# Branch sum, its norm, the output product, the residual and the third norm by halves of the tokens, in a macaron layer on one Trainium2 core

## What is computed

```
x = x + 0.5 * FFN(layernorm(x))
x = x + attention(layernorm(x))
x = x + 0.5 * FFN(layernorm(x))
```

```
w = softmax(logits / t); w = max(w, floor); w = w / w.sum(-1)
o = sum(w[..., i:i+1] * branches[i] for i in range(4))
o = o * rsqrt((o * o).mean(-1) + 1e-5) * onorm_w
x = x + o.reshape(b, l, 256) @ Wo
# then layernorm(x), the third norm, and the second FFN
```

## Time and profile before

| | us |
|---|---|
| median of 3 runs | 1204.77 (1200.77 to 1204.84) |
| the profiled execution | 1207.12 |
| its span, first to last instruction | 1205.4 |
| PE busy | 1053.0 (87%) |
| DVE busy | 821.7 (68%) |
| ACT busy | 548.9 (46%) |
| POOL busy | 414.4 (34%) |

### The profile page before, as it was taken

The page is one execution under the profiler, slowest core; times in us unless marked ns, Lnnn a source line. Parts: engine busy times, 40 slices in busy tenths (PEclk is TensorE's granted clock), DMA queues, the critical chain, the costliest instruction groups (busy, mean ns, idle before and its releaser), DMA issues.

```text
span 1205.4 us, 25681 instructions
## 1 busy us (share of the span) xinstructions
PE 1053.0 (87%) x10348; PEld 779.9 (65%) x10348; DVE 821.7 (68%) x1556; ACT 548.9 (46%) x965; POOL 414.4 (34%) x648
## 2 busy tenths in 40 slices
PE   3938898899989998899988998899988998897738
PEld 2823784488637884488637885488637885487427
DVE  6584477875787577875787667865787567863363
ACT  2244338443655337443564337443564337532322
POOL 8118200950058200951048300861048300860000
PEclk9968899999999999999999999999999999995758
DMA  5140104020220103020230203110130202120000
GB/s 156 19 105 2 35 18 96 11 52 2 69 55 11 43 19 89 18 48 6 51 74 3 51 19 73 33 35 20 44 80 1 53 1 68 39 51 3 1 0 18
DMA packets 82933, 47.45 MB, mean 39 GB/s; under 512 B 58496, under 2 KB 76416, under 8 KB 82816
## 3 DMA queue, kind: packets, MB, share of 16 engines
q1 hardware_dynamic: 82816, 45.82, 16.4%
HBM read 31.12 MB, written 14.68 MB: 38 GB/s over the span
## 4 chain that ended last, share of the span: by engine, by line
PE 59%; DVE 25%; ACT 7%; issue 4%; POOL 3%; DMA 1%; SPq 0%; DVEq 0%; ACTq 0%; POOLq 0%
PE psum L789 12%; PE psum L791 11%; PE psum L790 11%; DVE conv_acc L1374 6%; PE psum L820 4%; DVE arena L1607 3%; PE psum L982 3%; PE psum L967 3%; PE psum L1001 2%; PE psum L1006 2%; PE psum L1161 2%; ACT arena L587 2%; DVE arena L1609 2%; DVE f_fm L1504 1%; POOL l_prod L525 1%
## 5 line engine op out<-in xcount | busy, mean ns | idle before, releaser
L525 POOL TENSOR_TENSOR l_prod<-arena 64x30 f32<-64x30 f32 (+14 forms) x240 | 150.3, 626 | 568.5 <-DMA arena<-l_dram 550.3
L583 ACT ACTIVATE h_f<-psum,b_col 128x512 f32<-128x512 f32 x128 | 87.9, 688 | 209.4 <-PE psum L791 209.2
L529 POOL TENSOR_TENSOR arena<-arena,l_prod 64x30 f32<-64x30 f32 (+14 forms) x240 | 157.0, 654 | 18.8
L1088 PE MATMUL psum<-v_shift,fir_w 128*32 128x512 f32 x1152 | 143.9, 622 | 13.5 <-DVE wo_lo L1250 13.5
L789 PE MATMUL psum<-w_hi,h_hi 128*128 128x256 f32 x512 | 149.7, 292 | 0.0
L791 PE MATMUL psum<-w_hi,h_lo 128*128 128x256 f32 x512 | 143.6, 280 | 0.0
L790 PE MATMUL psum<-w_lo,h_hi 128*128 128x256 f32 x512 | 143.5, 280 | 0.0
L1374 DVE SCALAR_TENSOR_TENSOR conv_acc<-psum,conv_col,conv_acc 128x511 f32<-128x511 f32 x144 | 107.7, 748 | 32.0 <-ACT conv_acc L608 20.8
L789 PE MATMUL psum<-xt_hi,w_hi 128*128 128x512 f32 x256 | 109.6, 428 | 14.5 <-DVE b_half L1467 7.1
L1353 DVE CAST h_hi<-h_f 128x512 fp32r<-128x512 f32 x128 | 62.1, 485 | 88.1 <-PE psum L791 40.8
L820 PE MATMUL psum<-ident,arena 128*128 128x128 f32 x384 | 57.4, 298 | 54.7 <-DVE arena L1621 35.1
(11 more groups left out here) (232 smaller groups left out, 2198.3 us busy)
## 6 DMA issues: line engine op xcount, KB each, us to landing
x_in<-in_L_attn_x SPq DMA_DIRECT2D x8, 512.0 KB, 3.8
v_dram<-v_fm SPq DMA_DIRECT2D x16, 256.0 KB, 2.8
v_shift<-v_dram SPq DMA_DIRECT2D x16, 256.0 KB, 3.6
out<-x_tok SPq DMA_DIRECT2D x8, 512.0 KB, 2.9
v_shift<-v_dram SPq DMA_DIRECT2D x16, 255.5 KB, 4.4
v_shift<-v_dram SPq DMA_DIRECT2D x16, 255.0 KB, 5.2
v_shift<-v_dram SPq DMA_DIRECT2D x16, 254.5 KB, 5.8
arena<-in_L_ffn_w SPq DMA_DIRECT2D x2, 1024.0 KB, 7.2
```

The costliest lines, as they stand in the source:

```text
L525: pool.tensor_tensor(prod, l_inv[:, k + 1:, k:k + 1].broadcast_to(shape), l_inv[:, k:k + 1, 0:k].broadcast_to(shape), ALU.mult).then_inc(i ...
L529: pool.tensor_tensor(l_inv[:, k + 1:, 0:k], l_inv[:, k + 1:, 0:k], prod, ALU.add).then_inc(inverted, 1)
L583: act.activation(h_f[:, m % 2, :], bank, ACT.Gelu, bias=b1_col[:, m:m + 1]).then_inc(read, 1)
L1088: last = pe.matmul(fir[p][0][col:col + 32, :], fir_w[:, group, n - 1 if n else TAPG, :], v_shift[:, group, at_t:at_t + T], start=(n < 2), ...
```

## The change

The stage is cut by halves of the tokens (two tiles, 8 of 16 token-head units each), and each engine's list is put into a new order.

- VectorE: the four instructions of the weighted sum become eight of half the size, interleaved so that most need no wait for the one just before (`mark` only counts; the wait stands before the reader). Sum of squares, mean, reciprocal and normalisation are done for half 0, then half 1; the residual's statistics, variance, reciprocal and third norm likewise. The statistics of `x_in` are split: the four row statistics move up, before the wait for the exponential; aggregate and variance stand between the halves of the norm. `q_rows` moves behind the first `low_rows`, `q_inverse` behind the residual.
- ACT: square and root by halves; the root of the q sums moves behind the copies of v; the high rows of half 1 move behind the filter's copies; the third norm's root is taken per half, the first ahead of the last filter-tile copy, the second behind it.
- PE: the turn of half 0, then the last filter products and the turns of v, then the turn of half 1, the output product of half 0, three turns of filter tiles, the output product of half 1, the last filter tile.

```diff
-        DVE_STEPS = {"head": 49, "body": 82, "last": 77, "tail": 38}
+        DVE_STEPS = {"head": 49, "body": 90, "last": 85, "tail": 46}
...
 # ACT
                 if at.back:
-                    act.wait_ge(mix_made, i + 1)
-                    act.activation(sq_u, f_tok[:, :, 0, :], ACT.Square).then_inc(mix_squared, 1)
-                    act.wait_ge(onrm_made, i + 1)
-                    act.activation(onrm[:, :], onrm[:, :], ACT.Sqrt).then_inc(oroot_made, 1)
-                if at.front:
-                    act.wait_ge(qnrm_made, j + 1)
-                    act.activation(nrm[:, 1, :], nrm[:, 1, :], ACT.Sqrt).then_inc(qroot_made, 1)
-                if at.back:
-                    high_rows(at, 3, "mix_t")
+                    mix_square(at, 0)
+                    mix_root(at, 0)
+                    mix_square(at, 1)
+                    mix_root(at, 1)
+                    high_rows(at, 3, "mix_t", 0)
+                if at.next:
+                    root(0, j + 1)
                 if at.front:
                     for h in range(2, HEADS):
                         out_of(at, "fir", h, f_fm[:, h, :])
...
 # PE
+                if at.back:
+                    mixed_rows(0)
                 if at.front:
                     firs(at, 1, range(8, 9))
+                    to_tok(at, "v_t", lambda h: v_fm[:, h, :])
+                if at.back:
+                    mixed_rows(1)
+                    output(0)
+                if at.front:
                     copied(pe, at, "fir", HEADS - 1)
+                    for t in range(TILES - 1):
+                        fir_rows(t)
+                if at.back:
+                    output(1)
+                if at.front:
+                    fir_rows(TILES - 1)
                     off_diagonal(at, "lhalf")
...
 # VectorE
+                if at.next:
+                    dve.wait_ge(x_loaded, 16 * j + 32)
+                    x_rows = row_stats(x_in, range(TILES))
+                if at.back:
                     dve.wait_ge(exp_made, i + 1)
...
+                    weighted(f_tok, 0, 0)
+                    weighted_d = weighted(dv_tok, 2, 0)
+                    weighted(f_tok, 0, 1)
+                    summed = branch_sum(0, weighted_d)
+                    weighted_d = weighted(dv_tok, 2, 1)
+                    mixed(0, summed)
+                    summed = branch_sum(1, weighted_d)
+                    mean_square(0)
+                    mixed(1, summed)
+                    mix_normalise(0)
+                    mean_square(1)
+                if at.next:
+                    variances(0, range(TILES), x_rows)
+                if at.back:
+                    mix_normalise(1)
+                    low_rows(3, "mix_t", 0)
+                if at.front:
+                    q_rows()
+                if at.back:
+                    low_rows(3, "mix_t", 1)
+                if at.back:
+                    dve.wait_ge(x2_begun, i + 1)
+                    residual_rows(0)
+                    residual_rows(1)
+                if at.front:
+                    q_inverse()
+                if at.back:
+                    ln3_normalise(0)
+                    ln3_normalise(1)
+                    low_rows(2, "ln3", 0)
+                    low_rows(2, "ln3", 1)
```

More of the change, by code:

```diff
@@ L1177, in one_pass, with mixed_rows, output @@
                     firs(at, 1, range(0, 8))
+                def mixed_rows(b):
+                    pe.wait_ge(norm_made, 2 * i + b + 1)
+                    turn_tiles(at, "mix_t", b)
+                def output(b):
+                    copied(pe, at, "mix_t", b)
+                    bank, full = claim(pe, at, "wo", b)
+                    for t in (2 * b, 2 * b + 1):
+                        for k in range(HALVES):
+                            rows = slice(P * t, P * t + P)
+                            last = product3(pe, bank[:, C * (t % 2):C * (t % 2) + C], xt_hi[:, k, rows], xt_lo[:, k, rows],
+                                            wo_hi[:, k, :], wo_lo[:, k, :], k == 0, k == HALVES - 1)
+                    last.then_inc(full, 1)
@@ L1611, in one_pass @@
-                if at.front:
-                    q_rows()
-                if at.back:
-                    dve.wait_ge(mix_squared, i + 1)
-                    link(dve.tensor_reduce(oss[:, :], sq_u, AX.X, ALU.add))
-                    dve.tensor_scalar(onrm[:, :], oss[:, :], 1.0 / D, 1e-5, ALU.mult, ALU.add).then_inc(onrm_made, 1)
-                    dve.wait_ge(oroot_made, i + 1)
-                    link(dve.reciprocal(oinv[:, :], onrm[:, :]))
-                    for b in range(2):
-                        us = slice(2 * HEADS * b, 2 * HEADS * b + 2 * HEADS)
+                    units = [slice(2 * HEADS * b, 2 * HEADS * b + 2 * HEADS) for b in range(2)]
@@ L1621, in one_pass, with mix_normalise @@
+                    def mix_normalise(b):
+                        us = units[b]
+                        dve.wait_ge(oroot_made, 2 * i + b + 1)
+                        link(dve.reciprocal(oinv[:, us], onrm[:, us]))
                         dve.tensor_tensor(xn_u[:, us, :], f_tok[:, us, 0, :],
                                           oinv[:, us].unsqueeze(2).broadcast_to([P, 2 * HEADS, D]), ALU.mult).then_inc(norm_made, 1)
-                if at.front:
-                    q_inverse()
-                if at.back:
-                    low_rows(3, "mix_t")
@@ L1627, in one_pass, with residual_rows @@
-                if at.next:
-                    dve.wait_ge(x_loaded, 16 * j + 32)
-                    stats(0, x_in)
-                if at.back:
-                    dve.wait_ge(x2_begun, i + 1)
-                    for b in range(2):
+                    def residual_rows(b):
                         bank, read = arrive(dve, at, "wo", b)
@@ L1646, in one_pass @@
-                    dve.wait_ge(std_made[2], i + 1)
-                    link(dve.reciprocal(rstd[:, :], std[2]))
-                    for t in range(TILES):
-                        last = dve.tensor_scalar(xn_tok[:, t, :], x2_tok[:, t, :], mv[2][:, t, 0:1], rstd[:, t:t + 1],
-                                                 ALU.subtract, ALU.mult)
-                        if t % 2:
-                            last.then_inc(xn_made[2], 1)
-                    low_rows(2, "ln3")
+                        tiles = range(2 * b, 2 * b + 2)
@@ new lines, in residual_rows, with ln3_normalise @@
+                        variances(2, tiles, row_stats(x2_tok, tiles))
+                    def ln3_normalise(b):
+                        two = slice(2 * b, 2 * b + 2)
+                        dve.wait_ge(std_made[2], 2 * i + b + 1)
+                        link(dve.reciprocal(rstd[:, two], std[2][:, two]))
+                        for t in (2 * b, 2 * b + 1):
+                            last = dve.tensor_scalar(xn_tok[:, t, :], x2_tok[:, t, :], mv[2][:, t, 0:1], rstd[:, t:t + 1],
+                                                     ALU.subtract, ALU.mult)
+                        last.then_inc(xn_made[2], 1)
```

120 lines of the change are left out of this document (69 added, 51 removed).

## The result

The change makes the kernel slightly slower: a median of 1209.26 us (1206.8 to 1213.45, 13 runs) against 1204.77 (1200.77 to 1205.9, 13 runs) for the kernel before, a ratio of 1.0041 [1.0027, 1.0054]. The forecast was 1199.0, the range 1191 to 1209: the result lies 0.3 above the range, and on the other side of no change. The profiled execution of after took 1206.80 with a span of 1205.1, the lowest of its runs, while that of before took 1207.12 and stood above its median. The totals of the two profiles can therefore not be set against each other; their stretches can.

A forecast was written before the change was run, and what follows sets the result against it. The 28.8 us stage was taken as bound by DVE's list plus a few round trips. Six body passes -4.5, last pass +0.4 and tail -1.7 gave -5.8, forecasting 1199.0 us on the median's terms, range 1191 to 1209.

The forecast's parts named there:

- TensorE's clock: New PE gap before the third norm's turn may halve the clock: +1.0 us, taken for half the passes, +0.5 each.
- round trips: DVE's waits on PE and ACT in the stage fall from 2.85 to 0.85 us a body pass: -2.0.
- Statistics of x_in: Four row statistics, 1.39 us, move from the stage into the exponential's wait: -1.1 us a body pass.
- Halving, contention and early starts: DVE's stage, body pass: halved instructions +0.6 us, four more beside POOL +0.7, starting before the previous has drained -0.65.
- The rival of POOL in the way: Added DVE instructions each wait out a whole POOL instruction, 0.65 us: 1216, or 1209 without the clock's fall; chance 0.12.
- Doubled small things: Second sum of squares, reciprocals, mean, variance and aggregate on DVE in the stage: +1.2 us a body pass.
- DVE's list as the one bound: The 28.8 us stage is set by DVE's instructions plus a few trips through PE and ACT; forecast -1.25 a body pass.
- Tail and last pass: Tail, without POOL or other PE work: -1.7 us; last pass, with no x_in statistics to move: +0.4 us.
- The clock stays up: Rival: no granted-clock loss before the third norm and a shorter last trip, -12 us, 1193; chance 0.12.
- Second half sets the end: Rival: last turn and half 1's low part wait for the whole list; trips give 1.0, total -1.6, 1203; chance 0.11.
- Instructions count, waits don't: Rival: early starts of 0.11 us are not had, losing 0.65 in each of 8 backs, 5.2 more, 1204; chance 0.08.

The follow-up runs named there:

- e1: Changed kernel plus nine throwaway matmuls on PE ahead of the third norm's turns, filling the new gap; 1199.43 us, 0.9941 of the kernel before.
- e7: Kernel before, old order, plus filler matmuls before the gate's logits, the first turn and `lhalf`, and in the tail; 1199.89 us, 0.9952 of the kernel before.
- e5: Changed kernel with nine filler matmuls before the third norm's turns, but x_in's row statistics back between the norm's halves; 1204.98 us, 0.9993 of the kernel before.
- e3: Kernel before with only the four row statistics of x_in moved ahead of the exponential's wait; 1206.05 us, 1.0004 of the kernel before.
- e6: Changed kernel plus filler matmuls before the gate's logits, the first turn and the third norm, also in the tail; 1195.12 us, 0.992 of the kernel before.
- e10: Changed kernel with nine filler matmuls before the third norm's turns, without the 60 instructions of POOL's inverse; 1180.14 us, 0.9798 of the kernel before.
- e12: Kernel before without the 60 arithmetic instructions of POOL's triangular inverse, run for a profile; 1205.14 us.
- e2: Kernel before plus nine filler matmuls on PE before the first turn of the branch sum's norm; 1205.92 us, 0.9992 of the kernel before.
- e4: Changed kernel with the first attention product `at0` issued ahead of the third norm's turns instead of behind them; 1210.02 us, 1.0039 of the kernel before.

## Why the prediction was wrong, point by point

**TensorE's clock: the step that failed.** The prediction saw the new gap (2 to 2.5 us forecast, 2.63 measured) and that it was close to the one that cost the clock, but took +1.0 "for half of the passes, +0.5". In both profiles of after the clock fell at the third norm or the FFN's start in every one of the seven passes with front and back, and a fall cost 1.5: 0.6 in the stage and 0.96 in the FFN. The price was sized on the 1.9 us at 0.50 of the earlier trace rows, as if the lowered stretch ended with the stage. Two things were wrong in that. The 1.9 us are the window that was asked for; the grant was lowered for longer, as this wider window of the same pass of before shows:

```profile
498.30:501.70 3.40, 3.29 (x13) 1.29 (x14) 2.34 (x7) 1.29 (x3) 3.01 (x6) 0.50 0.02 5
```

And behind the new gap stands the FFN, where PE has no wait at all, so every slowed matmul lies on the path. 1.0 a pass too little makes 6 us, the whole of the forecast's gain of 5.8. e1, which takes the fall away, stands at 1199.4, below both kernels; without any price for the clock the prediction's sum gives 1204.8 - 5.8 - 7 x 0.5 = 1195.5. The 4 us between are in the terms that follow.

**What the old order already paid.** The sum was made against stages whose clock had also fallen, once behind the first turn and once behind the wait for the gate's logits, and a gain from shortening the first gap was not separated from a gain of the order. e7 separates them: the fillers alone shorten the old order's body pass from 136.34 and 135.86 to 135.31. Its second turned rows wait 0.27 instead of 0.75, since PE turns them at the full clock; part of the "round trips" was the clock.

**Statistics of x_in: right in the new order.** -1.1 forecast; the rows show all 1.39 hidden and no lateness in after, and e5 pays 0.9 a pass by the medians for putting them back. e3 shows that the reason given was incomplete: the work was on the path only once the output product comes early enough not to be waited for.

**Round trips: less than forecast.** The forecast was 2.85 to 0.85. The third pass alone nearly bears it out (2.85 to 1.03), but over the six body passes DVE's waits in the stage fall from 2.94 to 1.60, by 1.3, and with the clock held (e7 to e1) from 2.31 to 1.12, by 1.2. The wait for the second output product, taken at 0.1, is 0.33 to 0.50 in e1.

**Halving, contention and early starts: contention mis-sized.** +0.6 and -0.65 balance, as the tail shows (8.20 in before, 8.11 in after, with POOL idle). Beside POOL the eight halves cost 1.05 more than the four instructions (8.85 to 9.90, means of the six passes), where +0.65 was forecast. With the tail's -0.09 contention is 1.14 instead of 0.7, 0.29 for each added instruction instead of 0.17. The rival of POOL in the way put its limit at 0.5 and does not hold as a mechanism, although its milder number, 1209, was met.

**Doubled small things** were not measured apart. With the clock held, e7 to e6, the terms as measured are -1.4 for the statistics, +0.27 for weights that come later, -1.2 for trips (2.31 to 1.11), +1.2 for the halves (8.73 to 9.93) and the +1.2 forecast for the small things: +0.1, where the sums of a pass differ by +0.16.

**DVE's list as the one bound** was right in the main for the new order (e5, e10: what is added to or taken from it comes through, in e5 in part) and wrong for the old one (e3, e12: trips through PE and ACT step in at once). The forecast of -1.25 subtracted from a bound that was not the only one.

**Tail and last pass.** The tail's stage became 2.3 shorter (1.7 forecast). The last pass moved by -0.2 (means of both profiles of each kernel; +0.4 forecast).

**The other rivals.** "The clock stays up" fell on the clock. "Second half sets the end" expected 1.0 from the trips, and was nearer to the 1.2 to 1.3 that they gave than the forecast's 2.0. "Instructions count, waits don't": that the halves cost nothing in the tail speaks against it. There the advice of the Trainium skill, "VectorE: DVE Perf Modes", section "Rules for kernel authors", to count instructions rather than semaphores did not decide: eight took no longer than four. Beside POOL four more instructions did cost 1.1, but there it is POOL's turns between them that cost.

## What to carry to other kernels

Where a reordering shortens a stage, as here, look at what PE does in its new idle time and what stands behind it: a gap of 2.6 us in front of a stage where PE never waits cost more than the reordering saved, and nine throwaway matmuls into a bank that was about to be overwritten gave it back; four gave back under a third (1206.51). Compare two orders with the clock held in both, or one pays for gaps that the other has elsewhere. Cutting DVE's products with two SBUF inputs into halves was free only where POOL was idle. Take a mean over all passes, not the one pass that was looked at, and compare profiles only where they stand alike among the runs of their kernels.

## What the runs showed of the hardware

**The clock's fall follows PE's idle time, but not the length of one gap alone.** It fell behind waits of 2.67 (before), 2.63 (after) and 2.35 (e2), and in e4 behind three of 1.55, 0.74 and 1.58; not in e1 with 0.38, nor in before behind 1.53 and 0.59. But it did not fall behind a wait of 2.48 in the last pass of before, whose timeline and window are:

```profile
1042.07 0.66 PE L820 MATMUL psum<-ident,arena 128*128 128x128 f32 x4 [2.48 <-DVE arena L1621]
```

```profile
1042.00:1056.00 14.00, 11.33 (x120) 9.34 (x120) 10.05 (x23) 7.46 (x14) 12.51 (x20) 1.00 0.00 1
```

What decides between such cases these runs do not show. Filling one gap moves it to the next (e2), filling all of them gives 0.5% in the old order (e7) and, against after, 1.2% in the new one (e6, 1195.12 against 1209.26).

**POOL waits for DVE's whole instruction, DVE for a part of POOL's.** POOL's timeline in the third body pass of after, around the first product at 484.47:

```profile
484.43 0.42 POOL L529 TENSOR_TENSOR arena<-arena,l_prod 64x108 f32<-64x108 f32 x1
484.93 1.31 POOL L525 TENSOR_TENSOR l_prod<-arena 64x130 f32<-64x130 f32 x1
486.32 1.31 POOL L529 TENSOR_TENSOR arena<-arena,l_prod 64x130 f32<-64x130 f32 x1
```

and in before, around its first product of 2048 elements at 484.25:

```profile
484.20 0.45 POOL L525 TENSOR_TENSOR l_prod<-arena 64x130 f32<-64x130 f32 x1
484.73 2.39 POOL L529 TENSOR_TENSOR arena<-arena,l_prod 64x130 f32<-64x130 f32 x1
```

POOL's instruction of 0.45 becomes 1.31 beside products of 1.2 and 2.39 beside products of 2.31: it is let in once per DVE instruction. DVE pays less than POOL's own length: three products take 4.24 here and 3.49 in the tail, 0.25 more for each, beside POOL instructions that take some 0.45 by themselves. Beside POOL's copy in e10, 3.00 us long, a product takes 3.10. The Trainium skill, "SBUF — State Buffer", section "Who interferes with whom", says that the two shut each other out for a whole instruction; the numbers here agree for POOL's waits, and show a smaller price for DVE's. The prediction's 0.65 for "a whole POOL instruction" was the mistake: that mean contains POOL's own waiting, and DVE pays only a part of what is left. Which of POOL's instructions meets the products also matters. In the third pass of e6 POOL began late, with its smallest ones; from DVE's timeline there:

```profile
482.26 3.70 DVE L1674 TENSOR_TENSOR arena<-arena,mix_w 128x1024 f32<-128x1024 f32 x3
```

Three products took 3.70 instead of 4.24, the eight 8.99 instead of about 10.1, and the stage was 26.70, where that of e6's other body passes was 27.74 to 28.37.
